# First attention of a macaron block: VectorE's statistics in pieces, TensorE's small products in halves over two steps

## The reference, cut to what matters

```python
x = x + _L0_attn_ref(_layernorm(x, axis=-1), qkv_w, qkv_b, proj_w, proj_b)

def _L0_attn_ref(x, qkv_w, qkv_b, proj_w, proj_b):
    b, n, c = x.shape                      # 16, 512, 128; H = 16, D = 8
    qkv = x @ qkv_w + qkv_b
    q, k, v = jnp.moveaxis(qkv.reshape(b, n, 3, H, D), 2, 0)
    attn = jnp.einsum('bnhd,bmhd->bhnm', q, k) * scale
    attn = jax.nn.softmax(attn, axis=-1)
    out = jnp.einsum('bhnm,bmhd->bnhd', attn, v).reshape(b, n, c)
    return out @ proj_w + proj_b
```

## Time and profile before

| | us |
|---|---|
| median of 3 runs | 3902.61 (3892.71 to 3907.33) |
| the profiled execution | 3906.19 |
| its span | 3904.3 |
| first attention in it, first L928 to last group's end | about 538 to 1455 |
| full groups in it (VectorE's L693 at 635.75 to the one at 1339.53), 13 | 703.78, mean 54.1 |

### The profile page before, as it was taken

How to read it: one execution, slowest core, us unless ns; L and a number is a source line. 1 busy time by engine, 2 the same in 40 slices (tenths; PEclk the granted TensorE clock), 3 DMA queues, 4 the chain that set the end, 5 groups by cost and what they waited for, 6 DMA issues and landing times. The chain is left out here.

```text
span 3904.3 us, 46689 instructions
## 1 busy us (share of the span) xinstructions
PE 3191.1 (82%) x16333; PEld 1929.9 (49%) x16333; DVE 2762.0 (71%) x6734; ACT 1622.7 (42%) x2289; POOL 631.5 (16%) x555
## 2 busy tenths in 40 slices
PE   3999969999999987999766658888888888885763
PEld 2656633333333334565556545555555555553653
DVE  4777767877777737777557767776577777775576
ACT  1434316766666663343223323333333333332332
POOL 0000021111111000000012223233122112112222
PEclk9999957988898888999855579999899999997555
DMA  2000022211222100000100000000000000000001
GB/s 65 1 1 1 1 84 80 83 60 68 80 83 81 48 5 1 1 1 1 33 1 1 1 1 22 17 22 22 28 11 11 11 11 11 11 1 0 1 1 43
DMA packets 44915, 97.95 MB, mean 25 GB/s; under 512 B 12634, under 2 KB 16906, under 8 KB 40586
## 3 DMA queue, kind: packets, MB, share of 16 engines
q1 hardware_dynamic: 42506, 90.77, 6.6%
q10 hardware_dynamic: 2176, 4.19, 0.3%
HBM read 52.48 MB, written 42.47 MB: 24 GB/s over the span
## 5 line engine op out<-in xcount | busy, mean ns | idle before, releaser
L682 DVE TENSOR_REDUCE att_mx<-att_pair 128x2 f32<-128x1024 f32 x512 | 618.1, 1221 | 174.1 <-PE att_pair L928 173.4
L854 ACT ACTIVATE att_pt<-att_pair 128x1024 f32<-128x1024 f32 x512 | 522.7, 1025 | 272.2 <-PE att_pair L938 269.5
L950 PE MATMUL att_o<-att_pt,att_vx 128*32 128x256 f32 x4096 | 361.8, 442 | 9.7 <-ACT att_oT L860 5.7
L928 PE MATMUL att_pair<-att_k,att_q 24*128 24x512 f32 x1024 | 291.9, 574 | 44.1 <-DMA att_k<-att_spread_k 14.1
L938 PE MATMUL att_pair<-att_q,att_k 26*128 26x512 f32 x1024 | 281.1, 549 | 10.5 <-DVE att_mx L682 10.5
L938 PEld LDWEIGHTS att_pair<-att_q,att_k 26*128 26x128 f32 x1024 | 103.5, 200 | 226.1 <-issue 180.8
L435 ACT ACTIVATE ffnA_h<-ffnA_up,b 128x512 f32<-128x512 f32 x144 | 99.0, 688 | 222.4 <-PE ffnA_up L105 207.0
L435 ACT ACTIVATE ffnB_h<-ffnB_up,b 128x512 f32<-128x512 f32 x144 | 99.0, 688 | 222.1 <-PE ffnB_up L105 203.0
L950 PEld LDWEIGHTS att_o<-att_pt,att_vx 128*32 128x32 f32 x4096 | 95.2, 116 | 155.3 <-issue 136.0
L928 PEld LDWEIGHTS att_pair<-att_k,att_q 24*128 24x128 f32 x1024 | 107.2, 208 | 120.2 <-ACT att_pt L854 72.1
L2270 PE MATMUL att1q_acc<-att1q_qf,att1q_mem 128*128 128x512 f32 x256 | 133.7, 604 | 19.0 <-DVE att1q_qf L2036 17.6
(11 more groups left out here) (562 smaller groups left out, 8117.7 us busy)
## 6 DMA issues: line engine op xcount, KB each, us to landing
att_q<-att_spread_q SPq DMA_DIRECT2D x16, 1024.0 KB, 4.9
att_k<-att_spread_k SPq DMA_DIRECT2D x16, 1024.0 KB, 4.8
att_spread_q<-att_qhi SPq DMA_DIRECT2D x32, 256.0 KB, 2.5
att_spread_k<-att_khi SPq DMA_DIRECT2D x32, 256.0 KB, 3.4
context<-att1k_ctx SPq DMA_DIRECT2D x16, 512.0 KB, 2.6
att1q_cin<-context SPq DMA_DIRECT2D x16, 512.0 KB, 3.2
X<-L_attn_x ACTq DMA_DIRECT2D x8, 512.0 KB
att_spread_q<-att_qlo SPq DMA_DIRECT2D x16, 256.0 KB, 2.5
```

The source lines that it names most:

```text
L682: v.tensor_reduce(top[b % 2][:, t, h:h + 2], pair("s", k)[:, :].rearrange("p (h n) -> p h n", h=2), AX, ALU.max).then_inc(mx, 1)
L854: a.activation(pt[k % 8][:, :, :].rearrange("p h n -> p (h n)"), pair("t", k)[:, :], ACT.Exp, scale=scale).then_inc(p_, 1)
L928: last = pe.matmul(pair("s", k)[:, (j - j0) * 512:(j - j0 + 1) * 512], qb[b % 3][r, u, t * P:(t + 1) * P], kb[b % 3][r, u, :], start=True, ...
L950: last = pe.matmul(obank[j * BLOCK:(j + 1) * BLOCK, cols], vxb[b % 3][:, t, 4 * u + j, :], pt[(2 * g + j // 2) % 8][:, j % 2, cols], start ...
```

## The change

On VectorE `sums` becomes `stats` (the BN_STATS instructions, two at step 20 and two at step 22) and `moments` (the rest, at step 29). The maxima are taken with their sign turned, so that `maxima` needs two instructions in place of eight. `ended` moves from step 24 to 25, the first `divided` of a unit from 26 to 27.

On TensorE `turned` moves from step 5 to 4, `final` from 21 to 20, the `out` of step 25 to 26. `project_q` is cut into halves at the steps 9 and 10, `project_k` at 12 and 13, `project_v` at 17 and 18, `projected` at 23 and 24. On ScalarE `columns` moves from step 6 to 5, the q copy from 10 to 11, the v copy from 18 to 19.

```diff
+        def stats(b, t0, t1):
+            for t in range(t0, t1):
+                stated.at(v.bn_stats(nb.stats[b % 2][:, t, :], xg(b)[:, t, :]))
+        def moments(b):
+            v.wait_ge(stated.sem, TILES * (b + 1))
+            for t in range(TILES):
+                m = st.at(v.bn_aggr(nb.mv[b % 2][:, t, :], nb.stats[b % 2][:, t, :]))
...
-            for t in range(TILES):
-                m = st.at(v.tensor_scalar(rows[:, t, :, 0:8:2], tp[:, t, :, :], -1.0, None, ALU.mult))
-            v.wait_ge(st.sem, m)
-            for t in range(TILES):
-                last = v.scalar_tensor_tensor(rows[:, t, :, 1:8:2], tp[:, t, :, :], -1.0, rows[:, t, :, 0:8:2].bitcast(F32), ALU.mult, ALU.subtract)
-            last.then_inc(mt, 1)
+            m = st.at(v.tensor_copy(rows[:, :, :, 0:8:2], tp))
+            v.wait_ge(st.sem, m)
+            v.tensor_tensor(rows[:, :, :, 1:8:2], tp, rows[:, :, :, 0:8:2].bitcast(F32), ALU.subtract).then_inc(mt, 1)
...
+                if n == 20 and m + 2 < groups:
+                    stats(m + 2, 0, 2)
+                if n == 22 and m + 2 < groups:
+                    stats(m + 2, 2, TILES)
-                if n == 24 and old:
+                if n == 25 and old:
                     ended(m - 2)
-                if n == 26 and now:
+                if n == 27 and now:
                     divided(UNITS * (m - 1))
-                if n == 28 and m + 2 < groups:
-                    sums(m + 2)
+                if n == 29 and m + 2 < groups:
+                    moments(m + 2)
...
-                if n == 6 and new:
+                if n == 5 and new:
                     columns(m + 1)
-                if n == 10 and new:
+                if n == 11 and new:
                     raw_q(m + 1)
-                if n == 18 and new:
+                if n == 19 and new:
                     values(m + 1)
...
-                if n == 5 and new:
+                if n == 4 and new:
                     turned(m + 1)
-                if n == 9 and new:
-                    project_q(m + 1)
-                if n == 13 and new:
-                    project_k(m + 1)
+                if n in (9, 10) and new:
+                    project_q(m + 1, n - 9)
+                if n in (12, 13) and new:
+                    project_k(m + 1, n - 12)
-                if n == 17 and new:
-                    project_v(m + 1)
-                if n == 21 and old:
+                if n in (17, 18) and new:
+                    project_v(m + 1, n - 17)
+                if n == 20 and old:
                     final(m - 2)
-                if n == 23 and old:
-                    projected(m - 2)
-                if n == 25 and now:
+                if n in (23, 24) and old:
+                    projected(m - 2, n - 23)
+                if n == 26 and now:
                     out(UNITS * (m - 1))
```

More of the change, by code:

```diff
@@ L584, in attn0 @@
     wq, wk, wm, ones, fill = signals(nc, ctx, name, "wq wk wm ones fill")
-    st, zeroed, gs = Steps(nc, ctx, name + "_chain"), Steps(nc, ctx, name + "_zero"), Steps(nc, ctx, name + "_pool")
+    st, zeroed, gs, stated = [Steps(nc, ctx, name + n) for n in ("_chain", "_zero", "_pool", "_stats")]
     nb = NormBuffers(mem, 2)
@@ L674, in vector @@
     def vector(v):
-        def sums(b):
-            norm_stats(v, st, nb, b, xg(b), 1e-5, var)
+        def stats(b, t0, t1):
[6 more added lines that the diff above has]
+            v.wait_ge(st.sem, m)
+            v.tensor_scalar(nb.rstd[b % 2][:, :], nb.mv[b % 2][:, :, 1], 1e-5, None, ALU.add).then_inc(var, 1)
         def maxed(k):
@@ L681, in maxed @@
             v.wait_ge(s_, k + 1)
-            v.tensor_reduce(top[b % 2][:, t, h:h + 2], pair("s", k)[:, :].rearrange("p (h n) -> p h n", h=2), AX, ALU.max).then_inc(mx, 1)
+            v.tensor_reduce(top[b % 2][:, t, h:h + 2], pair("s", k)[:, :].rearrange("p (h n) -> p h n", h=2), AX, ALU.max, negate=True).then_inc(mx, 1)
         def maxima(b):
@@ L714, in ended @@
             v.tensor_tensor(xg(b), xg(b), group(misc[:, :]), ALU.add).then_inc(done, 1)
-        sums(0)
+        stats(0, 0, TILES)
+        moments(0)
         v.memset(pt[0][:, :, :], 1.0).then_inc(ones, 1)
@@ L724, in vector @@
                 if groups > 1:
-                    sums(1)
+                    stats(1, 0, TILES)
+                    moments(1)
         for m in range(groups + 2):
@@ L903, in turned, with project_q, project_k, project_v @@
             turn(pe, misc, group(xn[:, :]), ident).then_inc(xT, 1)
[L905 to L916, removed]
+        def project_q(b, h):
+            if h == 0:
+                pe.wait_ge(xc, b + 1)
+                misc_free(pe, "q", b)
+            cols = slice(h * HALF, (h + 1) * HALF)
+            project = pe.matmul(misc[:, cols], A["qkv"][:, 0:C], xcol[:, cols], start=True, stop=True)
+            if h:
+                project.then_inc(qp, 1)
+        def project_k(b, h):
+            if h == 0:
+                misc_free(pe, "k", b)
+            cols = slice(h * HALF, (h + 1) * HALF)
+            project = pe.matmul(misc[:, cols], A["qkv"][:, C:2 * C], xcol[:, cols], start=True, stop=True)
+            if h:
+                project.then_inc(kp, 1)
+        def project_v(b, h):
+            if h == 0:
+                misc_free(pe, "v", b)
+            for t in range(2 * h, 2 * h + 2):
                 last = pe.matmul(misc[:, t * P:(t + 1) * P], xcol[:, t * P:(t + 1) * P], A["qkv"][:, 2 * C:3 * C], start=True, stop=True)
-            last.then_inc(vp, 1)
+            if h:
+                last.then_inc(vp, 1)
         def scores(k):
@@ L968, in final, with projected @@
             turn(pe, misc, group(otok[b % 2][:, :]), ident).then_inc(fT, 1)
[L970 to L973, removed]
+        def projected(b, h):
+            if h == 0:
+                pe.wait_ge(fc, b + 1)
+                misc_free(pe, "proj", b)
+            for t in range(2 * h, 2 * h + 2):
                 last = pe.matmul(misc[:, t * P:(t + 1) * P], ocol[:, t * P:(t + 1) * P], A["proj"][:, :], start=True, stop=True)
-            last.then_inc(fp, 1)
+            if h:
+                last.then_inc(fp, 1)
         turned(0)
-        project_q(0)
-        project_k(0)
-        project_v(0)
+        project_q(0, 0)
+        project_q(0, 1)
+        project_k(0, 0)
+        project_k(0, 1)
+        project_v(0, 0)
+        project_v(0, 1)
         scores(0)
```

## The result

| | before | after |
|---|---|---|
| median, us | 3904.97 (3892.71 to 3925.58, 4 runs) | 3970.64 (3958.9 to 3982.09, 4 runs) |
| ratio, 95% interval | | 1.0163 (1.0103 to 1.0223) |
| span of the profiled execution | 3904.3 | 3957.7 |
| mean granted clock | 0.856 | 0.844 |

The changed kernel is 1.6% slower, 65.7 us by the medians; 3951 was forecast. These are the busy shares and the slices of the clock of the page after, which answer to the earlier trace rows.

What follows compares the result with a forecast made beforehand. TensorE, through its lost clock, was taken to bound the kernel. A group of 49.3 + 0.35 x 24.3 = 57.8 us, 3.7 more than 54.1, times 13 adds 48 us: 3951 us forecast, range 3850 to 4040.

Steps and rivals of the forecast that it cites:

- What bounds: Full groups before: TensorE is busiest and its clock falls behind step 29, typically 13.65 us of a group at half clock.
- The price of half clock: In a full group, each microsecond at half clock costs 0.35 us.
- full-clock group: A group wholly at full clock: 49.8 us before the change, 49.3 us with it.
- VectorE's pieces: Statistics split over steps 20, 22 and 29: the 0.79 us wait at step 30 goes, 0.5 us a group won.
- TensorE's halves: Four projections cut at 256 columns: nothing taken for extra passes (at most 0.6 us a group), almost nothing for hiding.
- The upper bound of 3.9 us a group: Most that seven jobs or halves moved from odd to even steps could gain by hiding under the next L928's wait.
- What the moves uncover: Steps 5 and 21 lose their transposes; TensorE idles 0.69 + 0.54 us at steps 6 and 7, clock falls twice a group.
- the mean over one short, two short and one long stretch: Half clock per group behind the uncovered steps: 13.65, 27.3 or 32 us, mean 24.3 us.
- The ends: Groups at the ends, outside the 13 full ones, were taken as unchanged.
- B: Rival: clock stays up at steps 5 and 21, fall at step 30 gone, 62 us less, 3841 us; chance 0.22.
- C: Rival: one short stretch a group stays, 54.1 us, 3903 us, also if VectorE is still late; chance 0.20.
- The signs: Half clock over 13.65 us a group, falls behind step 6 or 22, not 30; wrong if clock holds through over 1 us idle.

Runs made afterwards that it cites:

- cover29_fill: cover29 plus useless repeats of transposed scores in the last group's pass and the two passes behind it; 3829.93 us, ratio 0.9781 to the kernel before.
- vector_only: The kernel before with only VectorE's statistics pieces and shorter, sign-turned maxima, TensorE and ScalarE as before; 3866.97 us, ratio 0.9915.
- vector_early: vector_only with `moments` moved from step 29 to 23; 3884.12 us, ratio 0.9921 to the kernel before.
- after_cover: The changed kernel with `turned` back at step 5, `final` at 21 and `columns` at 6; 3887.83 us, ratio 0.9951 to the kernel before.
- cover29: vector_early with the `out` of step 25 at step 29, that of 30 at 31, and VectorE's `divided` at 30 and 1; 3846.82 us, ratio 0.9823.
- after_fill: The changed kernel with the transposed scores of steps 6 and 22 made twice, results unneeded; 3904.64 us, ratio 1.0007 to the kernel before.

## Why the prediction was right, point by point

**What bounds.** Held. The clock decides: with it at 1.00 throughout, cover29_fill issues more products than the kernel before (16415 against 16333) and is 2.2% faster.

**The price of half clock, 0.35 us per us.** Held. From after: a group of 51.70 us at 0.97 has 3.1 us of half clock, one of 58.20 at 0.82 has 21.0, and (58.20 - 51.70) / (21.0 - 3.1) = 0.36. The full-clock group of 49.8 us stands as a row in vector_only.

**VectorE's pieces.** Held in their sign. The 0.79 us at step 30 became 0.26, which is the half microsecond forecast. They bring 0.8% by themselves (vector_only and vector_early), more than the prediction's 0.5 us a group, because the half clock falls from 11.9 to 3.1 us a group with them. In a group at the full clock the 0.5 us do not show: 49.8 us was worked out for before, which has no such group to check it by, and 49.8 was measured in vector_only. Wrong was the 0.2 us for the first of the two instructions of `maxima`: it met GpSimd and took up to 1.24 us in vector_only, 0.79 in after. The runs put no loss on that.

**TensorE's halves.** Nothing was taken for them, and in the total after_cover against vector_only shows nothing that the intervals separate. But nothing was too little: at the full clock a group took 48.89 us with them and the small shifts, and 49.80 without, 0.9 us of gain. In after_cover falls at step 30 ate it up: the 13 groups took 664.9 us there and 661.2 in vector_only. The upper bound of 3.9 us a group is excluded.

**What the moves uncover.** The mechanism was right and its terms were mis-sized. Idle of 0.69 + 0.54 us was worked out for the steps 6 and 7; after has 0.88 + 0.24:

```profile
697.21 0.50 PE L949 MATMUL att_pair<-att_k,att_q 24*128 24x512 f32 x2 [0.88 <-ACT att_pt L865]
...
699.10 0.50 PE L949 MATMUL att_pair<-att_k,att_q 24*128 24x512 f32 x2 [0.24 <-ACT att_pt L865]
```

The second was over-estimated, since ScalarE came through its two copies sooner (this product starts 3.51 us after the step 5 begins, at 695.59, and not 3.66) and the products ahead of it ended later; the first was under-estimated because L959 starts early, as the one that ends at 722.28.

The half clock was put at 24.3 us a group and came out at 16.9. The step that failed is the mean over one short, two short and one long stretch. Step 6 lost the clock in two of the thirteen full groups only, and at step 22 the stretch was 3.4 or 6.8 us twice as often as 30.7. A stretch as short as 3.4 us was in none of the three cases. Step 30 was counted as cured, and five groups still fell there.

Against that the full-clock group was put at 49.3 us and is 51.70 - 0.35 x 3.1 = 50.6. The prediction let the waits that the moves uncover cost nothing at the full clock. The runs give them 1.0 us for `turned` and 0.4 us for `final`: 48.9 of after_cover + 1.4 = 50.3. So three terms of that group were off, the pieces by 0.5, the halves by -0.9 and the waits by 1.4, and partly cancel. Together: 50.6 + 0.35 x 16.9 = 56.5, measured 56.3, forecast 57.8. So the full groups cost 28 us and not 48.

**The ends.** "Groups at the ends are taken as unchanged" failed by 24.4 us in the profiled pair, and this is what brought the total back near the forecast. The total was hit within 20 us by two errors that cancel; that is luck. The medians lie 12 us further apart than the profiled executions, and which stage has these 12 us no trace shows. That the clock falls at the end is not a property of the changed kernel alone. Before and after have the same idle of 1.7 us behind step 5 of pass 16; the trace of before kept its clock there:

```profile
1399.14 0.64 PE L950 MATMUL att_o<-att_pt,att_vx 128*32 128x256 f32 x8 [1.69 <-ACT att_oT L860]
```

and that of after lost it:

```profile
1426.67 0.64 PE L971 MATMUL att_o<-att_pt,att_vx 128*32 128x256 f32 x8 [1.70 <-ACT att_oT L871]
```

**The rivals.** B (no fall, 3841) named about the right price for the other outcome, though by another change: cover29_fill, without any fall in these groups, took 3829.93. Its 3864 for one falling group in three has no sum beside it; one short stretch in each such group gives 3862. C's claim, that VectorE would still be late at step 30, is out: L959, which waits for the maxima, has no idle before it in the full groups of after. The row gives count, busy us, mean ns and, last, the idle us before it.

```profile
L959 PE MATMUL att_pair<-att_q,att_k 26*128 26x512 f32 x832 | 224.0, 545 | 0.0
```

**The signs.** Half clock over 13.65 us a group, a fall behind step 22 and no wait for the maxima at step 30 came as said. Two signs did not. The clock still fell at step 30 in five of the 13 full groups, in four of them behind 0.30 us of idle for ScalarE. And it held through the steps 6 and 7, with 0.88 + 0.24 us of idle, in eleven of the 13; "over 1 us of idle" was the prediction's own sign of being wrong. Step 22 fell each time with 0.87 us, so the sign was drawn on the wrong quantity: the sum of the idle does not rank these places.

**The rules.** The idle gaps behind which the clock fell are all under 1 us in the full groups, as in the earlier trace rows, and down to 0.26 us in vector_only. The Trainium skill, "TensorE: Matmul & The Clock Gate", section "Why this matters for your kernels", warns only of gaps several times as long; these runs do not agree. In cover29 a step filled with transposes kept the clock in all full groups, and in vector_early the same step without them lost it in five. The same page, in "Part 4: PE-mode transpose", says that the full clock does not engage for transposes; these runs speak against that too, for the FP32 ones here: four of them took 0.66 us at a granted clock of 1.00 (720.95 in after) and 1.12 us at 0.50 (743.01 there).

**What stays open.** What decides whether one gap of 0.87 us, or of 0.26, loses the clock and its like in the next group does not. Most groups of after repeat in threes, which speaks for where the gap lies in time and against chance alone, but no run here varied that by itself. No run separates the idle of a bare step from its lack of work either, since each job that was put there took away both. And of the change's small shifts (`out` to step 26, `ended`, `divided`, the copies) none was run alone.

## What to carry to other kernels

On a pipeline whose steps are uneven, put TensorE's small jobs into the steps that have the least work of their own, and look at each step, not at the length of each queue: three jobs one step earlier cost 2% here (1% in the kernel before), and covering the one bare step that was left gained 1%. Shortening an idle gap is not enough: at step 30 it went from 0.79 to 0.26 us, and six of 13 groups still fell. Where a stage ends and one of its streams runs out, useless repeats into a bank that is written anyway can be cheaper than the clock. When two placements differ by a step, look at the granted clock before you look at busy time; after_fill, with more work than the changed kernel, was the faster of the two.

## What the runs showed of the hardware that was not expected

- A VectorE copy of 128x64 from SBUF to SBUF waits for GpSimd: L700 took 1244 ns where it began 0.1 us behind GpSimd's addition of two SBUF tensors (1.27 us, L778) and ended with it, and 206 ns where the two did not meet. In the kernel before, L693 of `maxima` takes up to 1256 ns against 166 in the middle. VectorE's row maxima, which read PSUM, kept 1.22 us beside any GpSimd instruction. The Trainium skill, "GPSIMD Engine Reference", section "8. Key points", says that GpSimd shares its SBUF interfaces with VectorE and contends with VectorE's two-port modes; this trace agrees so far as the copy waits, and gives the price. It does not show in which mode the copy ran.
- A repeated pair of `again` products, on 26 rows each in two row groups, costs about 0.2 us when it follows its like at once, not another 0.43: one repeat takes the idle from 0.87 to 0.65 us in after_fill, and the row of ten products above lasts 1.20 us where a pair alone lasts 0.50, which is 0.18 for each of the four more.
- The half clock can last from 3.4 to 30.7 us behind gaps that look alike, of 0.87 us at step 22 in after.
